# Indirect scatters held in pairs by the first products, small jobs moved from VectorE to GpSimd, last reductions one round later

## The reference, cut to what matters

```python
# mixer: decayed running sums of cos/sin features, read out by queries
den = jnp.cumsum(p_w[..., 0], axis=1)
num_re = jnp.cumsum(pwb * re_k, axis=1)
num_im = jnp.cumsum(pwb * im_k, axis=1)
s_re, s_im = (num_re * inv), (num_im * inv)                # inv = 1 / den
out_re = jnp.sum(s_re * qr + s_im * qi, axis=-1)           # sum over M = 8
out_im = jnp.sum(s_im * qr - s_re * qi, axis=-1)
y = silu(y_re + y_im) @ W_out
x = layernorm(x + y)
# experts: two of 8 per token, and one shared expert
logits = flat @ router_w.T
topk_p, topk_i = jax.lax.top_k(softmax(logits), 2)
out = sum_e mlp_e(flat) * combine[:, e] + mlp_shared(flat) # mlp: square(relu(x W1)) W2
x = layernorm(x + out)
```

## Time and profile before

| what | value |
|---|---|
| median of 3 runs | 519.29 us (515.29 to 523.53) |
| the profiled execution's own time | 515.11 us |
| its span | 513.3 us |
| mean granted PE clock | 0.964 of full speed |
| PE busy | 455.7 us, 89% of the span |
| DVE, ACT, POOL busy | 356.8, 356.2, 301.0 us |

### The profile page before, as it was taken

One profiled execution on the slowest core, in us unless ns is written; L12 is line 12 of the kernel. 1 busy time (PEld: TensorE's weight loads), 2 busy tenths in 40 slices (PEclk: granted clock), 3 DMA queues, 4 the chain that ended last, 5 costly groups with the idle time before them and its releaser, 6 DMA issues.

```text
span 513.3 us, 7556 instructions
## 1 busy us (share of the span) xinstructions
PE 455.7 (89%) x2184; PEld 296.2 (58%) x2184; DVE 356.8 (70%) x825; ACT 356.2 (69%) x557; POOL 301.0 (59%) x264
## 2 busy tenths in 40 slices
PE   8997999999999888887497969759999999999983
PEld 5333444433433333455366747559999999899731
DVE  5798999999999999997567645253433334465246
ACT  3989899999999999635245546417666666566527
POOL 5745777877777878727465564512455555556421
PEclk9998999999999999999599988889999999999997
DMA  8031246654343432001011111131222221222095
GB/s 267 24 100 42 84 146 209 228 173 151 136 162 137 161 130 86 1 1 54 31 42 43 32 47 34 42 84 40 70 66 81 64 74 52 62 61 60 16 329 163
DMA packets 41192, 48.55 MB, mean 95 GB/s; under 512 B 5616, under 2 KB 25266, under 8 KB 41152
## 3 DMA queue, kind: packets, MB, share of 16 engines
q1 hardware_dynamic: 35792, 39.07, 23.3%
q0 software_dynamic: 5216, 8.70, 5.4%
q10 hardware_dynamic: 144, 0.31, 0.2%
HBM read 19.17 MB, written 29.11 MB: 94 GB/s over the span
## 4 chain that ended last, share of the span: by engine, by line
PE 42%; DVE 31%; issue 8%; ACT 8%; another core or an unknown queue 5%; POOL 3%; DMA 1%; DVEq 0%; SPq 0%; ACTq 0%; POOLq 0%
PE routed_ph L1446 13%; PE routed_po L1459 12%; DVE memory_y_raw L760 9%; DVE memory_prod L751 8%; PE memory_nsum L608 4%; DVE memory_feat L736 3%; PE dispatch_spo L968 2%; PE dispatch_sph L958 2%; ACT finish_xo L1660 2%; POOL memory_feat L491 1%; PE routed_px L1434 1%; PE memory_ph L592 1%; PE memory_pk L531 1%; POOL table_scratch L1137 1%
## 5 line engine op out<-in xcount | busy, mean ns | idle before, releaser
L491 POOL TENSOR_TENSOR memory_feat<-memory_feat,memory_p_tok 128x1024 f32<-128x1024 f32 x64 | 121.6, 1924 | 35.8 <-ACT memory_feat L386 31.8
L608 PE MATMUL memory_nsum<-memory_feat,tri 128*128 128x512 f32 x256 | 116.5, 597 | 5.8 <-POOL memory_feat L491 2.0
L1422 POOL DMA_INDIRECT pick_scratch<-routed_ob,routed_xg x71 | 71.6, 1009 | 78.1 <-DVE routed_ob L1543 55.6
L1137 POOL DMA_INDIRECT table_scratch<-dispatch_xrow,dispatch_slot x64 | 61.9, 967 | 46.8 <-DVE dispatch_slot L1240 24.0
L608 PEld LDWEIGHTS memory_nsum<-memory_feat,tri 128*128 128x128 f32 x256 | 47.1, 190 | 64.2 <-issue 60.1
L1492 ACT ACTIVATE routed_rel<-routed_ph 128x512 f32<-128x512 f32 x71 | 42.3, 597 | 47.8 <-PE routed_ph L1446 45.7
L1446 PE MATMUL routed_ph<-routed_xs,routed_w1c 128*128 128x256 f32 (+1 forms) x368 | 71.1, 337 | 2.0 <-ACT routed_xs L1483 1.2
L1459 PE MATMUL routed_po<-routed_w2c,routed_hid 128*128 128x128 f32 x568 | 71.3, 276 | 0.5 <-ACT routed_hid L1501 0.5
L1543 DVE TENSOR_SCALAR routed_ob<-routed_po,routed_xg 128x128 f32<-128x128 f32 x71 | 22.6, 348 | 69.8 <-issue 45.1
L751 DVE TENSOR_TENSOR memory_prod<-memory_nsum,memory_query 128x1024 f32<-128x1024 f32 x58 | 68.5, 1216 | 1.4 <-PE memory_nsum L608 1.3
L1459 PEld LDWEIGHTS routed_po<-routed_w2c,routed_hid 128*128 128x128 f32 x568 | 67.0, 192 | 1.2 <-ACT routed_hid L1501 0.7
(11 more groups left out here) (189 smaller groups left out, 649.7 us busy)
## 6 DMA issues: line engine op xcount, KB each, us to landing
table_scratch<-memory_blank SPq DMA_DIRECT2D x68, 260.0 KB, 2.6
finish_pick<-pick_scratch SPq DMA_DIRECT2D x16, 256.0 KB, 5.6
routed_xg<-table_scratch SPq DMA_DIRECT2D x25, 130.0 KB
w<-w_up SPq DMA_DIRECT2D x9, 256.0 KB, 2.8
w<-w_down SPq DMA_DIRECT2D x9, 256.0 KB, 3.1
x_tok<-x SPq DMA_DIRECT2D x4, 512.0 KB, 3.9
out<-finish_xo SPq DMA_DIRECT2D x7, 256.0 KB, 2.3
routed_xg<-table_scratch SPq DMA_DIRECT2D x21, 65.0 KB
```

Source lines behind the costliest of these rows:

```text
L491: nc.gpsimd.tensor_tensor(v, v, pv, ALU.mult).then_inc(wfeat_done, 1)
L608: last = nc.tensor.matmul(nsum[:, o:o + 512], tri[:], feat[:, i % U, h, q * 512:(q + 1) * 512], start=True, stop=True)
L1137: nc.gpsimd.indirect_dma_start(out=table, in_=xrow[:, r, n, :], in_offset=None, out_offset=bass.IndirectOffsetOnAxis(ap=slot[:, r, n:n + 1 ...
L1422: nc.gpsimd.indirect_dma_start(out=pick_dram, in_=ob[:, u, h, :], in_offset=None, out_offset=bass.IndirectOffsetOnAxis(ap=xg[:, t % XU, h, ...
```

## The change

It does six things.

1. Inside `scatter(g)` POOL waits on `up_done` before each pair of scatters (a tile's two): pair t waits for first product number 4(g - 1) + t + 3, counted from 1. That is `up(g - 1, 2)`, `up(g - 1, 3)`, `up(g, 0)` and `up(g, 1)`. Group 7 isn't held, and group 0 only in its last two pairs.
2. The two instructions that write token numbers into the rows (`tokens`) go from DVE, where they stood at tile 28, to POOL at tile 29. They wait until DVE's last `fraction` is done, and the first scatter waits for them.
3. POOL adds the two product halves of tiles 29 and 30 (`add_halves`, 128x1024 each) after its last `carry`; DVE's reductions of these tiles read 1024 elements a partition instead of 2048.
4. The reductions of tiles 29, 30 and 31 move from rounds 0, 1, 2 to rounds 1, 2, 3, and the `invert` and `scale_last` that follow from rounds 0 and 2 to rounds 1 and 3. `silu(6)` and `silu(7)` on ACT move from the ends of rounds 2 and 3 to the middles of rounds 3 and 4.
5. Groups 4 and 6 take their inverse root from the bits on DVE and no longer from POOL.
6. The power for group 2 stands after four scatters of group 0 instead of five.

```diff
-POWERS = (0, 1, 2, 4, 6)
+POWERS = (0, 1, 2)
...
+            def add_halves(i):
+                pool.wait_ge(prod_done, 2 * i + 2)
+                v = feat[:, (i - 1) % U]
+                nc.gpsimd.tensor_tensor(v[:, 0], v[:, 0], v[:, 1], ALU.add).then_inc(halves_added, 1)
+
             for i in range(NT):
                 weigh(i)
                 if i >= B:
                     carry(i)
+                if i == NT - 1:
+                    add_halves(NT - 3)
+                    add_halves(NT - 2)
                 tail(i)
...
-                nc.vector.tensor_reduce(y_raw[:, j % 2, b, :], products(i)[:, 0:2].rearrange("p h (c m) -> p c h m", m=M),
-                                        AX.XY, ALU.add).then_inc(red_done, 1)
+                if i in (NT - 3, NT - 2):
+                    dve.wait_ge(halves_added, i - (NT - 4))
+                    nc.vector.tensor_reduce(y_raw[:, j % 2, b, :], products(i)[:, 0].rearrange("p (c m) -> p c m", m=M),
+                                            AX.X, ALU.add).then_inc(red_done, 1)
+                else:
+                    nc.vector.tensor_reduce(y_raw[:, j % 2, b, :],
+                                            products(i)[:, 0:2].rearrange("p h (c m) -> p c h m", m=M),
+                                            AX.XY, ALU.add).then_inc(red_done, 1)
...
-    LAST_REDUCES = {0: NT - 3, 1: NT - 2, 2: NT - 1}
+    LAST_REDUCES = {1: NT - 3, 2: NT - 2, 3: NT - 1}
...
+                    if g in (3, 4):
+                        silu(g + 3)
                     relu(g, 2)
                     square(g, 2)
...
-                    if g in (2, 3):
-                        silu(g + 4)
...
                 if g == 0:
+                    pool.wait_ge(tokens_set, 2)
                     pool.wait_ge(mem.table_set, 16 * mem.fills)
-                for n in range(g * GT, (g + 1) * GT):
+                for t in range(GT):
+                    if t == 2 and g + 2 in POWERS:
+                        inverse_root(g + 2)
+                    if g < NG - 1 and (g - 1) * FC + t + 3 > 0:
+                        pool.wait_ge(up_done, (g - 1) * FC + t + 3)
+                    n = g * GT + t
                     for r in range(2):
-                        if n == g * GT + 2 and r == 1 and g + 2 in POWERS:
-                            inverse_root(g + 2)
                         nc.gpsimd.indirect_dma_start(
...
+            def tokens():
+                pool.wait_ge(mem.later_in, 48)
+                pool.wait_ge(mem.frac_done, NT)
+                for r in range(2):
+                    nc.gpsimd.tensor_scalar(xrow[:, r, :, D:D + 1].bitcast(U32), token.unsqueeze(2),
+                                            float(r * NTOK), None, ALU.add).then_inc(tokens_set, 1)
+
             def tail(i):
+                if i == NT - 3:
+                    tokens()
                 if i >= NT - 2:
                     inverse_root(i - (NT - 2))
...
                 elif i == NT - 4:
-                    tokens()
                     residual(0)
...
-                    if g == 0:
+                    if g == 1:
                         invert(TPB - 2)
                         scale_last(TPB - 2)
-                    elif g == 2:
+                    elif g == 3:
                         invert(TPB - 1)
                         scale_last(TPB - 1)
```

More of the change, by code:

```diff
@@ L291, in memory @@
         red_done = sem("red_done")
+        halves_added = sem("halves_added")
         y_done = sem("y_done")
@@ L851, in dispatch @@
         ones_set = sem("ones_set")
+        tokens_set = sem("tokens_set")
         silu_done = sem("silu_done")
@@ L1169, in constants @@
                 link(nc.vector.memset(used[:], 0.0))
-            def tokens():
-                for r in range(2):
-                    last = nc.vector.tensor_scalar(xrow[:, r, :, D:D + 1].bitcast(U32), token.unsqueeze(2),
-                                                   float(r * NTOK), None, ALU.add)
-                link(last)
             def residual(g):
```

## The result

The changed kernel takes 520.21 us (median of 22 runs, 514.92 to 528.9), the kernel before 517.31 us (22 runs): a ratio of 1.0081, 95% interval 1.0055 to 1.0106. So it is slightly slower where 505 us and a gain were forecast. The profiled execution took 522.35 us, span 520.5. It lies above its kernel's median and the profiled execution of the kernel before, 515.11 us, near the lower end of its own runs, so the two traces are 7.2 us apart where the medians are 2.9: they show where time goes and not how much the change costs.

What follows compares the result with a forecast made beforehand. It took unplaced semaphore waits, 27.6 us of the dispatch stage, put down to dense scatter bursts, as the bound. Terms 6.2 + 1.1 + 0.5 + 4 = 11.8 us off 515.1 gave 503.3; it named 505 us, range 492 to 514.

Steps and rivals of the forecast that it cites:

- what remains to be won is 24.7 us: Dispatch stage: unplaced waits left for the holds to reduce, 27.6 us less 2.9 us.
- round 1: Moving tile 29's put-off DVE work off the chain to rank(2): -6.2 us, from moved work, a shorter wait and the clock.
- later reductions: Tile 31's reduction, reciprocal and scaling moved to round 3, making residual(6) late instead of residual(5): 0, bounds -2 and +3.
- halves: POOL's two additions behind the last carry, hidden in its idle wait for group 1's variance: 0.
- Root(2): Group 2's root on POOL one scatter earlier, for which DVE waits in the dispatch stage: -1.1 us.
- Tokens: End of memory stage: token writes moved from DVE to POOL, 0.35 us each there: -0.5 us, bounds -1.4 and +0.7.
- bits: Groups 4 and 6: extra DVE instructions hidden in DVE's waits, POOL freed of two roots: 0, bounds -1 and +2.
- Holds: Dispatch stage: holds end scatter bursts sooner in three or four of seven held groups: -4 us, bounds 0 and 24.7.
- The rule against the holds: Skill rule that DMAs never contend with compute engines; by it bursts wouldn't delay relu or rank and holds give nothing.
- Holds do nothing: Rival: holds seldom bind or the delays have another cause; 507 to 512 us, chance 0.28.
- Bursts dissolve: Rival: PE and POOL fall into step and most unplaced waits vanish; 491 or 495 us, chance 0.17 (488 to 499).
- Scatters last: Rival: held scatters end the dispatch stage and delay the routed loads; 519 or 526 us, chance 0.07 (above 517).

Runs made afterwards that it cites:

- e7_pauses: The changed kernel without additions and holds, with an unneeded GpSimd power (1.04 us) behind every pair of scatters; 521.10 us, one run.
- e13_before_paused: The kernel before with only an unneeded GpSimd power of 4 elements behind every fourth scatter; 505.33 us, ratio 0.9780.
- e10_short_pauses: e9_pause_by_four with an addition of 4 elements behind every pair of scatters instead of the power behind every fourth scatter; 514.91 us, ratio 0.9928.
- e17_shorter_pause: e14_late_sums_paused with two additions of 2 elements in place of the power behind every fourth scatter; 514.66 us, ratio 0.9968.
- e18_pause_by_eight: e14_late_sums_paused with the power behind every eighth scatter only; 517.98 us, ratio 0.9964.
- e5_only_holds: The kernel before with only the holds of scatter pairs added; 515.80 us, ratio 0.9987.
- e6_early_sums: e1_full_sums with the sums of tiles 29 to 31, their scalings, silu(6) and silu(7) back in their earlier rounds; 514.52 us, ratio 0.9897.
- e1_full_sums: The changed kernel without GpSimd's additions of product halves, DVE summing tiles 29 and 30 in full; 516.23 us, ratio 0.9989.
- e3_later_sums: The kernel before with only the sums of tiles 29 to 31, their scalings, silu(6) and silu(7) a round later; 522.80 us, ratio 1.0114.
- e14_late_sums_paused: e9_pause_by_four with the last sums a round later, as in the change; 504.30 us, ratio 0.9749.
- e9_pause_by_four: e6_early_sums without holds, with an unneeded GpSimd power of 4 elements (1.04 us) behind every fourth scatter; 504.88 us, ratio 0.9761.
- e16_halves_paused: e9_pause_by_four with GpSimd's two additions of product halves and DVE's shorter sums of tiles 29 and 30; 508.59 us, ratio 0.9836.
- e11_longer_early: e8_longer_holds with the last sums in the rounds of the kernel before; 509.10 us, ratio 0.9837.
- e8_longer_holds: e1_full_sums with each pair of scatters held one first product longer and the last group held too; 506.59 us, ratio 0.9760.
- e12_pool_roots: e6_early_sums with the roots of groups 4 and 6 on GpSimd again; 518.79 us, ratio 0.9846.
- e2_no_holds: The changed kernel without the holds of scatter pairs, nothing else changed; 528.73 us, ratio 1.0203.

## Why the prediction was wrong, step by step

**The cause** of the unplaced waits was taken for dense bursts "by coincidence in time". The runs now show it: with all scatters put off the rounds are 16 us shorter; with all of them there but paused the waits are gone (e7_pauses, e13_before_paused). What exactly is held up inside the chip while a row runs wasn't measured. Nor is it shown whether the length of a row counts or the mean rate. By the starts in the traces, a scatter comes every 1.27 us in an unbroken row, every 1.32 in e10_short_pauses, 1.33 in e17_shorter_pause, 1.39 in e18_pause_by_eight, 1.52 in the four kernels with a pause behind every fourth, and 1.78 in e7_pauses; in these five cases of a pause 48.6, 32.3, 40.4, 0 to 4.2, and 0 us are unplaced. A limit on the rate, somewhere between 1.39 and 1.52 us a scatter, fits as well as a limit on the row. A gap of 0.56 us behind every single scatter would tell them apart; it wasn't run.

**The step that failed is the way the sum is built, and in it two terms.** It took the unplaced waits as an amount from which edits subtract ("what remains to be won is 24.7 us", of which the holds take 4), and priced the other edits on a schedule in which they stay where they are. They don't. Each edit moves the times of the slots, and these decide which groups are issued without a stop between them. The prediction did count that six scatters would still go out in one row; it didn't ask what happens in group 7, which isn't held, once its slots are ready in time. There the 14.4 us wait arose.

The ratios to the kernel before show which terms it was. They make a ladder from it to the changed kernel: with the holds 0.9987 (e5_only_holds), with tokens, bits and the place of root(2) besides 0.9897 (e6_early_sums), with the later sums besides 0.9989 (e1_full_sums), with the additions besides 1.0081. In us of 515 these steps are -0.7, -4.6, +4.7 and +4.7, each uncertain by 3 to 5 us; the last is clear of that, the third barely, the others not. The prediction had -4, -1.6, -6.2 (round 1 and the later reductions together) and 0. So the terms that turned the sign are *round 1*, forecast at -6.2 and measured at +4.7 in this order and at +1.1% alone (e3_later_sums), and *halves*, forecast at 0 and measured at +4.7.

*Round 1, -6.2 us.* Right as a piece of PE's path once the rows are broken, lost in the whole. With the rows broken it is 3.0 us between turn_x(1) and turn_x(3) (e14_late_sums_paused 21.58, e9_pause_by_four 24.59), and the clock of that window is 1.00 instead of 0.61; I had 3.8 for the moved work and 1 for the clock. In the changed kernel the piece from turn_x(1) to turn_x(3) is 26.3 us where it was 28.8, and 0.7 of these 2.5 us are root(2)'s; the rest of the gain went into late semaphores ahead of residual(3) and the router's copy (2.06 and 4.21 us). Alone, the edit cost 1.1%.

*Root(2), -1.1 us.* From turn_x(1) to turn_x(2) 8.19 us before, 7.46 after: 0.7.

*Tokens, -0.5 us.* 0.38 us each on GpSimd (I took 0.35), root(0) 0.53 us sooner. But in both kernels DVE's first Newton step ends only with the weighing that GpSimd runs beside it (217.52 and 217.50 before, 217.24 and 217.21 now), so the step takes 1.07 us instead of 0.56 and ends 0.28 us sooner, and turn_x(0) in e1_full_sums is only 0.2 us early.

*Halves, 0.* Mis-sized by 2.7 us at its place and some 4 us in the whole (e1_full_sums, e16_halves_paused). I asked whether GpSimd had idle time and not what DVE does in that time. The trace shows an addition of 2.60 us holding four scalings of 1.12 us until it ends, while beside the second addition DVE's residual (0.68 us) and statistics (0.87) keep their time and only the small scaling that makes the variance takes 0.50 us instead of 0.17. The Trainium skill (SBUF — State Buffer, Who interferes with whom) says this of a DVE instruction in a two-port mode, which a scaling can enter: whoever issues first gets the pair of ports that DVE and GpSimd share for the whole instruction, and the other blocks. The trace agrees with it, 3.94 us instead of 1.12, but no run shows in which mode these scalings ran. I had used that section and missed that line. DVE's two short sums take 1.22 us each instead of 2.28, so of the 2.2 us expected of them 2.1 were had, and they bought nothing that can be seen.

*Later reductions, 0, and bits, 0.* Tile 31's reduction, reciprocal and scaling take 3.9 us in round 3 (3.8 counted). With e11_longer_early against e8_longer_holds and e9_pause_by_four against e14_late_sums_paused the move as a whole, round 1's gain included, measured 2.5 and 0.6 us better where late semaphores are fewer; neither is clear of the intervals. The bits stay open (e12_pool_roots).

*Holds, -4 us.* In the changed kernel they give 6 to 8.5 us, in the kernel before nothing that can be told. The term was neither too large nor too small but no constant. Two small slips stand in it: the smallest of the eight pieces besides the one of 0.84 us is 2.62 us and not 2.89, and 2.9 us are taken off for a wait of which only 1.4 were counted as won. Neither moves the forecast.

**The rule against the holds** (the Trainium skill, SBUF — State Buffer, Who interferes with whom: a DMA never contends with a compute engine) didn't decide: where scatters stand in long rows, the news of PE's, ACT's and DVE's work is late. The rule is about ports, and semaphores are not in it. The rule on dense increments (the Trainium skill, VectorE: DVE Perf Modes, The TRN2 errata) pointed the right way in asking for space between them; what the runs show is lateness, not a deadlock, and no run shows that increments are what is too dense.

**The rivals.** "Holds do nothing" is refuted for the changed kernel by e2_no_holds; the time it named, 507 to 512, missed too. "Bursts dissolve" is what e13_before_paused shows, but at 505 us and not 491 to 495: 15 gaps of 1.26 us instead of 0.30 are 14.4 us more on GpSimd, which becomes the bound. "Scatters last" had a time close to the result and the wrong mechanism: the last scatter ended at 333.02, 3.5 us sooner than before, and the load waited for the table behind DVE.

**The best version** is e14_late_sums_paused, 504.30 us, 2.5% under the kernel before; e9_pause_by_four, e13_before_paused and e8_longer_holds aren't told apart from it. It keeps tokens, bits, root(2) and the later sums, drops the additions and the holds, and has the pause.

## What to carry to other kernels

Where GpSimd issues indirect DMAs in a row and engines wait for releasers that the profile can't place, try a pause of a microsecond behind every few of them before tuning anything else, and measure other edits only then: under late semaphores an edit that shortens the path can measure as a loss, as the later sums did here. One kernel shows this; how long and how often the pause has to be is to be tried again in another. A wait that holds work back until an event cuts rows only where the event is late; check the place where it isn't applied. Before moving work into another engine's idle time, look at what the other engines do then: here DVE's scalings stood as long as GpSimd's addition ran.

## What the runs showed that I hadn't expected

Eight scatters at 0.96 us with 0.30 us between are too many in a row even if 1.26 us follow, four are few enough; with 0.53 us behind four (e17_shorter_pause) or 0.37 us behind each pair (e10_short_pauses) 32.3 and 48.6 us of unplaced waits stay, where the kernel before has 45.6. During a row of 16 the news of a finished product came 14.4 us late, and was there 2.9 us after the last scatter. Even DVE's own steps can wait for each other: at 254.20 in the changed kernel, just behind two of the scatters, one Newton step waits 1.04 us for the step before it, where 0.04 us lie between such steps elsewhere. A power of 4 elements takes GpSimd 1.04 us and an addition of as many 0.22 us, which is what made the first a useful pause.
